# A four-layer cross-attention kernel: the first norm, the context set-up and the weight folds of its launch in another order

## What is computed

```python
# block 0: gated linear recurrence, attention over the context, MLP
x_norm = x * norm1_scale * rsqrt(mean(x*x, -1) + 1e-6)
q, k, v, z = (x_norm @ W + b for W, b in the four pairs)
gamma = clip(sigmoid(gelu(z @ Wg1 + bg1) @ Wg2 + bg2)
             * sigmoid(gelu(k @ Wgc1 + bgc1) @ Wgc2 + bgc2), 1e-6, 1 - 1e-6)
gate = sigmoid(z_t @ Wgz + bgz + h_prev @ Wgh + bgh)       # step t of S = 1024
h_t = (1 - gate) * h_prev + gate * z_t + g_t * h_prev
qh = q @ Awq + abq;  kh = ctx @ Awk + abk;  vh = ctx @ Awv + abv
x = x + h_seq + softmax_attention(qh, kh, vh) @ Awo + abo + 0.1 * v
x = x + mlp(rms(x, norm2_scale))
# block 1: attention of layernorm(x) over layernorm(ctx), then a 4-wide MLP over 256 features
norm_X = layernorm(ctx, norm1_w, norm1_b)
```

## Time and profile before

| what | value |
|---|---|
| median of 3 runs | 958.37 us (957.61 to 959.52) |
| the profiled execution | 956.19 us, of which the span from the first to the last instruction is 954.4 us |
| PE busy | 859.4 us, 90% of the span |
| DVE busy | 519.0 us, 54% |
| ACT busy | 455.5 us, 48% |
| POOL busy | 46.4 us, 5% |
| chain that ended last | PE 71%, ACT 14%, DVE 12%, issue 2%, DMA 1% |
| mean granted TensorE clock | 0.952 |

### The profile page before, as it was taken

One profiled execution on the slowest core, in us unless ns is written; L12 is line 12 of the kernel. 1 busy time (PEld: TensorE's weight loads), 2 busy tenths in 40 slices (PEclk: granted clock), 3 DMA queues, 4 the chain that ended last, 5 costly groups with the idle time before them and its releaser, 6 DMA issues.

```text
span 954.4 us, 10850 instructions
## 1 busy us (share of the span) xinstructions
PE 859.4 (90%) x4452; PEld 402.2 (42%) x4452; DVE 519.0 (54%) x716; ACT 455.5 (48%) x678; POOL 46.4 (5%) x39
## 2 busy tenths in 40 slices
PE   3988799989999999987799999999888999889987
PEld 2533344443444444534233625333355434554342
DVE  2456999923343103225853516268959677894542
ACT  3576322274343323525354251458777368852534
POOL 0000000020000000000300000000002000220000
PEclk9899999998979999998799799899979999999999
DMA  8000200000000000011000000000000000000011
GB/s 321 1 1 0 89 0 0 0 1 1 0 1 1 0 1 0 1 66 65 0 1 1 2 1 1 1 1 0 1 1 1 1 0 1 1 1 1 2 45 45
DMA packets 3007, 15.64 MB, mean 16 GB/s; under 512 B 656, under 2 KB 912, under 8 KB 2320
## 3 DMA queue, kind: packets, MB, share of 16 engines
q1 hardware_dynamic: 2816, 12.88, 3.5%
q0 software_dynamic: 144, 2.10, 0.5%
HBM read 12.87 MB, written 2.10 MB: 16 GB/s over the span
## 4 chain that ended last, share of the span: by engine, by line
PE 71%; ACT 14%; DVE 12%; issue 2%; DMA 1%; DVEq 0%; SPq 0%; POOL 0%; ACTq 0%
PE ps L410 69%; ACT AR L626 3%; DVE VB L639 3%; ACT AR L1763 2%; ACT AR L1753 1%; DMA CX<-in_ctxT 1%; DVE AR L2039 1%; DVE VB L1895 1%; DVE AR L508 1%; PE ps L585 1%; DVE AR L651 1%; ACT AR L1729 1%; ACT AR L631 1%; ACT AR L629 1%; ACT AR L1470 1%
## 5 line engine op out<-in xcount | busy, mean ns | idle before, releaser
L410 PE MATMUL ps<-AR,WA 128*128 128x512 f32 (+3 forms) x780 | 340.3, 597 | 12.0 <-DVE AR L2272 3.6
L410 PEld LDWEIGHTS ps<-AR,WA 128*128 128x128 f32 (+2 forms) x780 | 143.6, 190 | 194.7 <-issue 181.0
L410 PE MATMUL ps<-AR,CN 128*128 128x512 f32 (+3 forms) x320 | 115.4, 614 | 7.4 <-DVE AR L503 2.6
L410 PE MATMUL ps<-AR 128*64 128x128 f32 (+5 forms) x680 | 98.9, 408 | 9.8 <-DVE AR L2039 2.6
L651 DVE TENSOR_TENSOR AR<-ps,AR 128x512 f32<-128x512 f32 x24 | 16.6, 692 | 104.0 <-ACT AR L631 104.0
L410 PEld LDWEIGHTS ps<-AR 128*64 128x64 f32 (+4 forms) x680 | 53.1, 164 | 46.9 <-issue 21.5
L626 ACT ACTIVATE AR<-ps 77x2048 f32<-77x2048 f32 x24 | 44.0, 1868 | 59.4 <-PE ps L410 59.4
L410 PEld LDWEIGHTS ps<-AR,CN 128*128 128x128 f32 (+2 forms) x320 | 40.3, 166 | 60.2 <-issue 39.6
L639 DVE TENSOR_REDUCE VB<-ps 128x16 f32<-128x1232 f32 x32 | 45.0, 1439 | 34.0 <-PE ps L410 34.0
L410 PE MATMUL ps<-KB,WA 128*128 128x512 f32 (+1 forms) x120 | 53.0, 609 | 0.9 <-ACT AR L1746 0.9
L2169 DVE SCALAR_TENSOR_TENSOR AR<-AR,VC 128x512 f32<-128x512 f32 x72 | 50.6, 749 | 5.3 <-ACT AR L1687 4.4
(11 more groups left out here) (326 smaller groups left out, 1068.8 us busy)
## 6 DMA issues: line engine op xcount, KB each, us to landing
WA<-in_m SPq DMA_DIRECT2D x1, 2856.0 KB, 9.6
WA<-in_m SPq DMA_DIRECT2D x1, 2560.0 KB, 15.7
X<-in_xT POOLq DMA_DIRECT2D x1, 2048.0 KB, 9.4
WA<-in_m SPq DMA_DIRECT2D x1, 2048.0 KB, 7.4
out<-X SPq DMA_DIRECT2D x4, 512.0 KB, 3.1
WB<-in_m SPq DMA_DIRECT2D x1, 1024.0 KB, 18.2
AR<-in_rows SPq DMA_DIRECT2D x1, 640.0 KB, 10.1
WA<-in_m SPq DMA_DIRECT2D x1, 512.0 KB, 16.5
```

Of the source, the lines that this page charges most:

```text
L410: return nc.tensor.matmul(out, lhsT, rhs, start=first, stop=last)
```

## The change

The input norm's steps are woven into the context set-up: ACT squares units 0 and 1 ahead of the centred context and units 2 and 3 behind it, PE takes the mean squares in two pairs between the context's own products, DVE norms units 0 and 1 ahead of the write-back of the gate fold and units 2 and 3 behind it. The table of `Ln` and `Exp` is loaded once, at the start. The z loop waits in its first turn for two normed units, no longer for four. Much of the context set-up (`E1`, `ECA`, `ECB`, the normed context `NXS`) goes behind the norm on DVE. POOL scales `Wz` and `Wv`. The query fold, its eight one-column bias products and the `fc1T` product go from the launch into `memory()`, in the middle of the first narrow sweep, and with them ACT gets the write-back of `CQ` and DVE that of `NF` and the bias columns, ahead of that sweep in their streams. `WB` is loaded later. The core of the diff:

```diff
             sp.dma_start(WA[:, 0:a], m0[:, 0:a]).then_inc(sem("ld_kv0"), 16)
-            sp.dma_start(WB[:, :], m2).then_inc(sem("ld_w12"), 16)
...
             sp.wait_ge(*after("h", 8 * (SWEEPS_BF + 1)))
+            sp.dma_start(WB[:, :], m2).then_inc(sem("ld_w12"), 16)
...
         def _(pool):
             nc.gpsimd.dma_start(X[:, :, :, :].rearrange("p c b s -> p (c b s)"), xT).then_inc(sem("ld_x"), 16)
+            pool.wait_ge(*after("ld_vec", 16))
+            pool.wait_ge(*after("ld_w0", 16))
+            for k in range(2):
+                nc.gpsimd.tensor_scalar(w("Wz", 2)[:, k, :], w("Wz", 2)[:, k, :], v("n1", k), None, ALU.mult).then_inc(sem("wz"), 1)
+            for k in range(2):
+                nc.gpsimd.tensor_scalar(w("Wv", 2)[:, k, :], w("Wv", 2)[:, k, :], v("n1", k), 0.1, ALU.mult, ALU.mult).then_inc(sem("wz"), 1)
...
+            def mean_square1(q):
+
+                pe.wait_ge(*after("norm_sqs", NORMS["r1"] + q + 1))
+                mm(ps[:, R1_BANK[q], :], cn("mean"), SQR1[q][:, 0, :]).then_inc(sem("norm_ms"), 1)
...
+            pe.wait_ge(*after("wz", 2))
+            pe.wait_ge(*after("wready", 1))
+            pe.wait_ge(*after("norm_ln", NORMS["r1"] + B * J))
             pe.wait_ge(*after("g6", 2))
-            pe.wait_ge(*after("nf", 1))
...
             with pe.Fori(0, J) as j:
                 pe.wait_ge(*after("gam", j * 8))
-                pe.wait_ge(*after("norm_xn", NORMS["r1"] + B * J))
+                pe.wait_ge(*after("norm_xn", NORMS["r1"] + n2(j, 1)))
                 lin_pe(pe, "z_mm", j, w("Wz", 2), lambda b, c: XN[:, c, b, tj(j)], (2, 3))
+                pe.wait_ge(*after("cn_ln", 1))
...
             def memory():
                 pe.wait_ge(*after("ld_kv0", 16))
+                for mo in range(DC):
+                    for c in range(DC):
+                        mm(ps[:, 3, T - 4 + mo:T - 3 + mo], feat(w("Awq", 2), c, mo), v("bq", c), c == 0, c == DC - 1)
+                    for c in range(DC):
+                        mm(ps[:, 3, T - 2 + mo:T - 1 + mo], feat(w("Awo", 2), c, mo), v("abv0", c), c == 0, c == DC - 1)
+                pe.wait_ge(*after("nxs", 2))
+                for b in BS:
+                    for c in range(DC):
+                        last = mm(ps[0:M, 2, T - 16 + 8 * b:T - 12 + 8 * b], NXS[:, c, b * M:(b + 1) * M], VC[:, vcol["fc1T"][0] + 4 * c:vcol["fc1T"][0] + 4 * c + 4], c == 0, c == DC - 1)
+                last.then_inc(sem("nf_mm"), 1)
                 keys_pe(pe, "a0", w("Awk", 2))
                 values_pe(pe, "a0", w("Awv", 2))
+                for m in range(DC):
+                    for c in range(DC):
+                        last = mm(ps[:, 7, m * D:(m + 1) * D], w("WqT", 2)[:, c, m * P:(m + 1) * P], w("Awq", 2)[:, c, :], c == 0, c == DC - 1)
+                last.then_inc(sem("cq_mm"), 1)
                 pe.wait_ge(*after("kv_kb", KEYS["a0"] + 2))
                 pe.wait_ge(*after("kv_vs", LAYER["a0"] + 1))
+                pe.wait_ge(*after("nf", 1))
+                pe.wait_ge(*after("cq", 1))
...
             prep_act(act, "a0")
+            act.wait_ge(*after("cq_mm", 1))
+            for k in range(DC):
+                ins = nc.scalar.activation(CQ[:, k, :], ps[:, 7, k * D:(k + 1) * D], ACT.Copy, scale=v("n1", k))
+            ins.then_inc(sem("cq"), 1)
```

More of the change, by code:

```diff
@@ L269, in xattn_stack_kernel @@
         SQR1 = SQ + [c1b.take(DC, T) for _ in range(B)]
-        RTR1 = RT + GG
+        RTR1 = RT + [OPG[:, 0, b, 0:T] for b in range(B)]
         c1c = Carver(DC * B * S)
@@ L1430, in _, with squares1, roots1 @@
             act.wait_ge(*after("ld_vec", 16))
+            def squares1(q):
+                b, span = part_of(q)
+                nc.scalar.activation(SQR1[q], X[:, :, b, span], ACT.Square).then_inc(sem("norm_sq"), 1)
+            def roots1(q):
+                act.wait_ge(*after("norm_ms", NORMS["r1"] + q + 1))
+                nc.scalar.activation(RTR1[q], ps[:, R1_BANK[q], :], ACT.Ln, bias=cn("eps6")).then_inc(sem("norm_ln"), 1)
+                act.wait_ge(*after("norm_ln", NORMS["r1"] + q + 1))
+                nc.scalar.activation(RTR1[q], RTR1[q], ACT.Exp, scale=-0.5).then_inc(sem("norm_rt"), 1)
+            nc.scalar.preload_act_table_set("natural_log_exp_and_others")
+            act.wait_ge(*after("ld_x", 16))
+            for q in UNITS[:B]:
+                squares1(q)
             act.wait_ge(*after("cn_xc", 1))
             nc.scalar.activation(CSQ, CXC, ACT.Square).then_inc(sem("cn_sq"), 1)
+            for q in UNITS[B:]:
+                squares1(q)
+            for q in UNITS[:B]:
+                roots1(q)
             for t, k in ((FT6, 6), (ET6, 7)):
@@ L1435, in _ @@
                 nc.scalar.activation(t, ps[:, k, 0:DC * P].rearrange("p (c n) -> p c n", c=DC), ACT.Copy).then_inc(sem("ft6"), 1)
-            nc.scalar.preload_act_table_set("natural_log_exp_and_others")
+            for q in UNITS[B:]:
+                roots1(q)
+            act.wait_ge(*after("g6_mm", 2))
+            nc.scalar.activation(GS, ps[:, 7, 0:P], ACT.Copy, scale=D ** -0.5).then_inc(sem("g6"), 1)
             act.wait_ge(*after("cn_ms", 1))
@@ L1808, in _, with sums1, normed1 @@
             TT(CXC, CX[:, :, :], bc(ps[:, 4, 0:B * M], DC, 1), ALU.subtract).then_inc(sem("cn_xc"), 1)
+            def sums1(q):
+                dve.wait_ge(*after("norm_sq", NORMS["r1"] + q + 1))
+                TT(SQR1[q][:, 0], SQR1[q][:, 0], SQR1[q][:, 1], ALU.add).then_inc(sem("norm_sqs"), 1)
+            def normed1(q):
+                b, span = part_of(q)
+                dve.wait_ge(*after("norm_rt", NORMS["r1"] + q + 1))
+                TT(XN[:, :, b, span], X[:, :, b, span], bc(RTR1[q], DC, 1), ALU.mult).then_inc(sem("norm_xn"), 1)
+            dve.wait_ge(*after("ld_x", 16))
+            for q in UNITS[:B]:
+                sums1(q)
             dve.wait_ge(*after("ld_r6", 16))
@@ L1815, in _ @@
             TT(E6, E6, R6[:, 2, :], ALU.add).then_inc(sem("e6"), 1)
+            for q in UNITS[B:]:
+                sums1(q)
+            for q in UNITS[:B]:
+                normed1(q)
+            dve.wait_ge(*after("pw", 3))
+            for k in range(2):
+                TS(CG[:, k, 0:P], ps[:, 2, k * P:(k + 1) * P], v("n1", k), None, ALU.mult)
+            ch.link(TT(cb("gcb"), ps[:, 2, 2 * P:2 * P + 1], v("bg1c"), ALU.add))
+            dve.sem_inc(sem("wready"), 1)
+            dve.wait_ge(*after("g6_mm", 1))
+            STT(out=G6, in0=ps[:, 6, 0:P], scalar=1.0 / D, in1=cn("same"), op0=ALU.mult, op1=ALU.mult).then_inc(sem("g6"), 1)
+            for q in UNITS[B:]:
+                normed1(q)
             dve.wait_ge(*after("e6", 1))
```

78 lines of the change are left out of this document (25 added, 53 removed).

## The result

| | median | lowest to highest | runs |
|---|---|---|---|
| changed kernel | 949.41 us | 942.57 to 951.47 | 9 |
| kernel before, in the same comparisons | 957.86 us | 953.17 to 959.86 | 9 |

What follows compares the result with a forecast made beforehand. From 36.54 us the z loop was PE's own unbroken work, so its start set the total; in the first narrow sweep DVE was the bound. -10.7 - 0.8 + 4.0 = -7.5 us, 958.4 to 950.9; range 947.5 to 955.5.

Steps and rivals of the forecast that it cites:

- Start of the z loop: Launch: the new order starts PE's z loop at 25.8 instead of 36.54 us, -10.7 us; bounds -5.4 and -12.
- DVE's rest hidden: Launch: DVE's shifted work of some 6 us ends near 32, before its first gate input at 35.6 or more.
- POOL's scaling: Launch: the two scalings the z loop needs run from 18.3 to 19.9, or 24.7 at worst; costed at nothing.
- that rule: SBUF exclusion of DVE and GpSimd in the launch: two normings end at 24 instead of 21; sum -10.2 for -10.7.
- Clock of the z loop: Z loop: less time at half clock at its start, gain between 0 and 1.6 us, taken as -0.8.
- The narrow sweep: First narrow sweep: moved work delays DVE's first product by 4.0 us; bounds +2.4 and +9.8.
- The sum: Whole kernel: z loop start, its clock and first narrow sweep together give -7.5 us, 950.9 us; chance 0.64.
- The slower one: Rival: narrow products keep PE's clock down in launch and sweep, +4.4 us, 962.8 us; chance 0.05.
- the half-clock one: Rival: PE at half clock through the whole launch, -1.4 us, 957.0 us; chance 0.12.
- Gain taken up elsewhere: Rival: DVE's shifted rest or POOL ends the wait for the z loop, 958.4 us; chance 0.04.
- Full clock at both places: Rival: PE at full clock in launch and narrow sweep, -9.9 us, 948.5 us; chance 0.15.

Runs made afterwards that it cites:

- the third of the changed kernel: Changed kernel profiled again without edit, in a later comparison beside the kernel before; median 949.37 us, ratio 0.9918.
- the one on DVE: Changed kernel with the scaling of Wz and Wv on DVE instead of POOL; one run, 945.93 us.
- the first profile: First profiled execution of the changed kernel, no further edit; 949.32 us.
- the second: Changed kernel run and profiled again without edit; median 949.91 us, ratio 0.9891.
- the fillers: Seven unread products in PE's second-block set-up pauses, added to the changed kernel with query-fold copies behind sigmoids, values first and four unread launch products; 942.90 us.
- warmed: Changed kernel plus four unread PE products in the launch, three of them while PE waits for the context; 948.25 us, ratio 0.9890.

## Why the prediction was right, step by step

- **Start of the z loop, -10.7 forecast.** Measured 25.10, 23.98 and 24.76 for 25.8: -11.4 to -12.6. X at 10.57 (10.7), mean squares of units 0 and 1 from 13.45 (13.6), the inverse roots, the hidden normings and the last releaser `GS` came as stepped through. Over-sized were the narrow products: the eight one-column records took 0.41 us, not 0.9. Their weights are only 64 columns wide; sixteen with 128 columns took 1.84 us, 0.115 each. The 0.114 that I took from the row of 24 was a mean over both widths in a stretch in which the clock fell; in the kernel with the fold back in the launch the same 24 took 2.23 us.
- **DVE's rest hidden.** It is: DVE had idled 7.60 us when the first gate input came at 37.56.
- **POOL's scaling, 18.3 to 19.9.** It ended at 21.6. Of the first pair (`Wz`) the first scaling took 2.00 us beside a norming of DVE, the second 0.92 with DVE idle, near my lower bound of 0.8; the two of `Wv` took 0.49 and 0.48. I had read "together they lose little" out of the earlier trace rows and set it against SBUF — State Buffer of the Trainium skill, section "SBUF: two separate sides". Where DVE is first (18.66 for 18.68), this trace agrees with that section: DVE loses nothing (1.23 us; 1.22 for the unit before), and POOL about the length of the norming. Where POOL is first, four profiles disagree with it. In the third of the changed kernel POOL's scaling ran from 18.60 to 19.53; by that section DVE's norming, begun at 18.83, would wait until 19.53 and end, by my estimate, near 20.8. It took 1.31 us and ended at 20.1, and POOL's second scaling beside it took 1.42 for 0.92. In the four profiles DVE took 1.28 to 1.35 us. So the sum by that rule, -10.2, didn't come. The scaling was hidden, as the one on DVE shows. The rows, POOL of the first profile and DVE of the third:

```profile
20.67 0.92 POOL L747 TENSOR_SCALAR WA<-WA,VC 128x256 f32<-128x256 f32 x1
```

```profile
18.83 1.31 DVE L1859 TENSOR_TENSOR AR<-X,AR 128x1024 f32<-128x1024 f32 x1 [0.48 <-ACT AR L1462]
```

- **Clock of the z loop, -0.8.** The means hide two opposite things. The loop started at full clock, which gave all of the 1.55 us; but the clock fell again behind PE's pause of 2.79 us at the head of the second turn and gave 1.8 back, together +0.3 in the first profile (rows below). The third has its fall at 25.0 instead. That a fall may just move is what my term missed; its size of +0.3 is just outside my bounds of -1.6 to 0.

The windows of the changed kernel around that fall (columns as above):

```profile
48.00:50.00 2.00, 0.95 (x2) 0.49 (x3) 1.85 (x3) 1.36 (x3) 0.00 (x0) 0.95 0.00 0
50.00:52.00 2.00, 2.00 (x4) 0.77 (x3) 1.81 (x4) 0.60 (x1) 0.00 (x0) 0.50 0.00 0
...
54.00:56.00 2.00, 2.00 (x7) 0.80 (x6) 2.00 (x3) 1.87 (x3) 0.00 (x0) 1.00 0.00 0
```

PE waits for half of the first, runs 4 records in the second at 0.50, and 7 in the last at 1.00.

- **The narrow sweep, +4.0 (2.4 to 9.8).** +2.1 in two profiles and +3.8 in one. The mechanism is shown by removal: with the copies behind the sigmoids the distance falls by 2.0 (both at half clock), with the values first too it is 12.4 for 14.1 (both at full clock), nearly that of before. PE's memory part was 7.0 us at full clock for 7.4. In the first profile the narrow products at its head didn't bring the clock down: 79.68 to 81.5 ran at the pace of 0.115 us each, and no fall followed before 203 us. In the second the clock fell at 81.7, behind them; whether they brought that about isn't shown. Of the twelve profiles with the fold in this place five have that fall.
- **The sum.** At the place of the last term it was -9.1 for -7.5 in the first profile (-11.4 + 0.3 + 2.1), -8.7 and -9.4 in the others. Between there and the end are two things that weren't in it, both of the clock. The fall at 118 us in the kernel before doesn't happen in the first and third profiles after, which raised the lead by 1.7; the second has one at 109. And behind 413 us the rest is 530 or 534 us in the same kernel. By medians 8.4 us remain. That they lie within 1 us of the forecast is in part luck: the start gave 0.7 to 1.9 us more than its term, the clock of the z loop took 0 to 0.3 where I had it give 0.8, the sweep cost 0.2 to 1.9 less, and in the first profile 10.6 us of lead shrank to 7.0 behind the last place that I had costed.
- **Rivals.** The slower one and the half-clock one are refuted by the start at 24 to 25 in all three profiles of the changed kernel. "Gain taken up elsewhere" is refuted by the 7.60 us. "Full clock at both places" (-9.9), to which I gave 0.15, is what the first profile shows at the two places and what the local milestones come nearest to; the median lies about halfway between it and the forecast.

What stays open: no run takes the woven norm alone out of the changed kernel, so its share is what is left when the fold, the halved wait, POOL's scaling and `WB` have been undone one by one, and not a difference of its own. Open too are why the clock falls at one place in one execution and 10 or 100 us away in the next, and whether the fillers or chance made the last kernel's runs lie close.

## What to carry to other kernels

Work moved out of a launch pays where the engine it leaves is the bound of the launch, and costs at the other place less by its duration than by what stands behind its copies in another engine's queue: put the copies behind that work, and the long products first. The same move gave nothing alone and 1.3 to 2.2 us of work together with the new order (4 to 5 us up to the sweep in one profile, of which the clock was the larger part), so undo parts from the changed kernel, not only add them to the old, and check what the clock did in between. And where the same kernel scatters by 1%, judge an edit by distances between two pieces of work in the traces, and run the kernel itself again before explaining a stretch far from the edit.

## What the hardware showed unexpectedly

The profile's granted clock reads 1.00 from the start to the first recorded fall, also where PE plainly ran at half pace. A window of the changed kernel:

```profile
14.00:16.00 2.00, 2.00 (x3) 0.67 (x2) 1.86 (x7) 1.62 (x3) 0.00 (x0) 1.00 1.03 430
```

The mean squares that run through this stretch took 3.78 us for four records at a clock of "1.00"; warmed, the same four took 1.98. At a program's head the clock is to be read from durations.

The part behind the first block took 526.7 to 526.9 us in three profiles, 529.8 to 530.8 in five and 533.9 to 534.3 in six, with nothing between, for kernels that there do the same work (one has seven products more). The same kernel was seen at two of these levels. For the same 3046 records PE was busy for 480.4 us at 534.3 (mean granted clock 0.93) and for 470.3 us at 526.8 (0.96). That is up to 7.6 us, nearly as much as the whole change gave.
